# A feed-forward loop on one core: row statistics over pairs of rows, and 0.01 tanh added by VectorE instead of TensorE

## What is computed

```python
def step(h, _):
    h = h + 0.01 * jnp.tanh(h)
    h = h * jax.nn.sigmoid(h)
    h = _layernorm(h, ln_w, ln_b)
    h = jnp.einsum('bsc,dc->bsd', h, W) + b
    return (h, None)
x, _ = jax.lax.scan(step, _layernorm(h2), None, length=30)
out = h2 + x
```

## Time and profile before

| what | us |
|---|---|
| median of 3 runs | 2138.03 |
| lowest and highest of the 3 | 2136.45, 2356.8 |
| span of the profiled execution, first to last instruction | 2132.7 |
| last stage, from its first DVE operation to the span's end | 461.1 |

### The profile page before, as it was taken

The page is one execution under the profiler, slowest core; times in us unless marked ns, Lnnn a source line. Parts: engine busy times, 40 slices in busy tenths (PEclk is TensorE's granted clock), DMA queues, the critical chain, the costliest instruction groups (busy, mean ns, idle before and its releaser), DMA issues. The chain is left out here.

```text
span 2132.7 us, 61654 instructions
## 1 busy us (share of the span) xinstructions
PE 1903.4 (89%) x20166; PEld 1487.2 (70%) x20166; DVE 1674.5 (79%) x4836; ACT 1153.7 (54%) x2296; POOL 484.8 (23%) x431
## 2 busy tenths in 40 slices
PE   2316399999999999999999999999957799999998
PEld 2315277777777777777777777777747477777776
DVE  3205388888888888888888888888865788888887
ACT  0103266666666666666666666666614366666665
POOL 5000000000000000000000000000004699999997
PEclk9999699999999999999999999999987799999999
DMA  3333100000000000000000000000041100000000
GB/s 111 75 71 63 44 3 3 3 3 3 3 3 3 3 3 3 3 3 3 3 3 3 3 3 3 3 3 3 3 95 32 29 0 0 0 0 0 0 0 30
DMA packets 38153, 33.35 MB, mean 16 GB/s; under 512 B 13781, under 2 KB 35477, under 8 KB 37141
## 3 DMA queue, kind: packets, MB, share of 16 engines
q1 hardware_dynamic: 36159, 32.21, 6.4%
q10 hardware_dynamic: 1972, 0.86, 0.2%
HBM read 22.02 MB, written 11.03 MB: 15 GB/s over the span
## 5 line engine op out<-in xcount | busy, mean ns | idle before, releaser
L614 ACT ACTIVATE z1hi<-ps 128x375 f16<-128x375 f32 x820 | 398.7, 486 | 405.1 <-PE ps L556 405.1
L554 PE MATMUL ps<-AThi,y0hi 125*128 125x150 f16 x2460 | 567.1, 241 | 36.5 <-DVE z1lo L650 34.6
L555 PE MATMUL ps<-ATlo,y0hi 125*128 125x150 f16 x2460 | 584.9, 238 | 0.0
L650 DVE TENSOR_TENSOR z1lo<-ps,z1hi 128x375 f16<-128x375 f32 x820 | 445.8, 544 | 171.3 <-ACT z1hi L614 171.2
L556 PE MATMUL ps<-AThi,y0lo 125*128 125x150 f16 x2460 | 564.8, 239 | 0.0
L655 DVE TENSOR_TENSOR y<-ps,negb 125x384 f32<-125x384 f32 x820 | 451.1, 550 | 37.2 <-PE ps L571 37.2
L569 PE MATMUL ps<-W1hi,z1hi 128*128 128x128 f16 x2460 | 455.2, 219 | 0.2 <-DVE y L655 0.2
L571 PE MATMUL ps<-W1hi,z1lo 128*128 128x128 f16 x2460 | 454.1, 219 | 0.0
L570 PE MATMUL ps<-W1lo,z1hi 128*128 128x128 f16 x2460 | 453.6, 219 | 0.0
L645 DVE SCALAR_TENSOR_TENSOR y0lo<-ps,y0hi 125x512 f16<-125x512 f32 x615 | 420.7, 684 | 1.1 <-ACT y0hi L610 1.1
L610 ACT ACTIVATE y0hi<-ps 125x512 f16<-125x512 f32 x615 | 363.4, 591 | 13.4 <-PE ps L536 13.4
(11 more groups left out here) (197 smaller groups left out, 2315.4 us busy)
## 6 DMA issues: line engine op xcount, KB each, us to landing
pooled_parts<-stage SPq DMA_DIRECT2D x410, 4.0 KB
zk<-z_parts SPq DMA_DIRECT2D x16, 360.4 KB
parts<-pooled_parts SPq DMA_DIRECT2D x16, 256.0 KB, 5.7
xs<-in_x_v SPq DMA_DIRECT2D x3, 1201.2 KB
xs<-in_x_v SPq DMA_DIRECT2D x5, 720.7 KB
z_parts<-zp SPq DMA_DIRECT2D x20, 180.2 KB
pooled_parts<-stage SPq DMA_DIRECT2D x205, 2.0 KB
pooled_parts<-stage SPq DMA_DIRECT2D x205, 10.0 KB
```

Source lines behind the costliest of these rows:

```text
L554: nc.tensor.matmul(o, hi, ahi, start=(ph == 0), stop=False, skip_group_check=True)
L555: nc.tensor.matmul(o, hi, alo, start=False, stop=False, skip_group_check=True)
L614: nc.scalar.activation(z1hi[:, q, 0:GV], ps[:, Z1B + q % 2, 0:GV], ACT.Identity).then_inc(z1hi_done, 1)
L650: nc.vector.tensor_tensor(z1lo[:, q, 0:GV], ps[:, Z1B + q % 2, 0:GV], z1hi[:, q, 0:GV], ALU.subtract).then_inc(z1lo_done, 1)
```

## The change

The statistics of two rows are taken by one `bn_stats` over 128 numbers, read in turns from the one row and the other, so that the even places are the one row and the odd places the other. Its six numbers are then the two rows' own mean and sum of squared deviations, and one `tensor_scalar` adds 64 eps. The three small operations go, and `sm` in the first six steps. POOL has only the power left. The 0.01 tanh is added on DVE, in place in PSUM, between gn and the statistics of a step; PE's matmul with `pct` and `pct` itself go. `y_ready` becomes two semaphores, for even and odd chunks. The first waits of a buffer's reuse are put on other semaphores accordingly.

```diff
--- before.py
+++ after.py
@@ tokens @@
...
                 v_.memset(ones[:], 1.0)
-                v_.tensor_scalar(pct[:], ident[:], 0.01, None, ALU.mult)
...
@@ feed_forward @@
-        sm = sb("sm", [P, 2, CR])
-
-        bs, bs0 = (sb(f"bn_parts{i}", [P, 2, CR, 6]) for i in range(2))
-        dm, dm0 = (sb(f"dm_{i}", [P, 2, CR]) for i in range(2))
-        s2, s20 = (sb(f"s2_{i}", [P, 2, CR]) for i in range(2))
-        q2, q20 = (sb(f"q2_{i}", [P, 2, CR]) for i in range(2))
+        bs, bs0 = (sb(f"bn_pairs{i}", [P, 2, CP, 6]) for i in range(2))
...
-        y_ready = sem("y_ready")
+        y_ready = [sem("y_ready_even"), sem("y_ready_odd")]
...
+        def squares(pairs, b):
+            return pairs[:, b].rearrange("p j (i k) -> p (j i) k", i=2)[:, :, 2]
+
+        def means(pairs, b):
+            return pairs[:, b].rearrange("p j (i k) -> p (j i) k", i=2)[:, :, 1]
...
@@ gpsimd @@
-                def inverse_roots(s2, q2, var, rs, b, n, added, rooted):
-
-                    nc.gpsimd.tensor_tensor(var[:, b, :], s2[:, b, :], q2[:, b, :], ALU.add).then_inc(added, 1)
-                    pool.wait_ge(added, n + 1)
-                    nc.gpsimd.tensor_tensor(rs[:, b, :], var[:, b, :], expo[:], ALU.pow).then_inc(rooted, 1)
...
-                        pool.wait_ge(parts_done, 2 * n + 2)
+                        pool.wait_ge(var_done, n + 1)
                         if late(n, 2):
                             pool.wait_ge(gn_done, n - 1)
-                        inverse_roots(s2, q2, var, rs, b, n, var_done, rs_done)
+                        nc.gpsimd.tensor_tensor(rs[:, b, :], var[:, b, :], expo[:], ALU.pow).then_inc(rs_done, 1)
...
@@ scalar @@
-                            act.wait_ge(y_ready, s - 1)
+                            act.wait_ge(y_ready[c % 2], half(2) + 1)
...
-                        act.wait_ge(y_ready, n + 1)
+                        act.wait_ge(y_ready[cn % 2], half(1) + 1)
...
@@ tensor @@
-                    if on(0):
-                        pe.wait_ge(th_done, s + 1)
-                        nc.tensor.matmul(ps[:, c, :], pct[:], th[:, c % 2, :], start=False, stop=True,
-                                         skip_group_check=True).then_inc(y_ready, 1)
...
@@ vector @@
-                def statistics(bs, dm, s2, q2, b, n, diffs, made, bns):
-
+                def statistics(src, pairs, var, b, n, bns, made):
+
+                    for j in range(CP):
+                        last = v_.bn_stats(pairs[:, b, j, :], src[:, 2 * j:2 * j + 2, :].rearrange("p i d -> p d i"))
+                    last.then_inc(bns, 1)
                     dve.wait_ge(bns, n + 1)
-                    v_.tensor_tensor(dm[:, b, :], bs[:, b, :, 1], bs[:, b, :, 4], ALU.subtract).then_inc(diffs, 1)
-
-                    v_.scalar_tensor_tensor(s2[:, b, :], bs[:, b, :, 2], D * EPS, bs[:, b, :, 5], ALU.add,
-                                            ALU.add).then_inc(made, 1)
-                    dve.wait_ge(diffs, n + 1)
-                    v_.scalar_tensor_tensor(q2[:, b, :], dm[:, b, :], D / 4.0, dm[:, b, :], ALU.mult,
-                                            ALU.mult).then_inc(made, 1)
+                    v_.tensor_scalar(var[:, b, :], squares(pairs, b), D * EPS, None, ALU.add).then_inc(made, 1)
...
                     dve.wait_ge(h2_loaded, (c + 1) * 16)
                     if c >= 2:
-                        dve.wait_ge(var0_done, c - 1)
-                    for r in range(CR):
-                        last = v_.bn_stats(bs0[:, b, r, :], h2[:, c, r * D:(r + 1) * D])
-                    last.then_inc(bn0, 1)
-                    statistics(bs0, dm0, s20, q20, b, c, diff0, parts0_done, bn0)
-                    v_.tensor_tensor(sm[:, b, :], bs0[:, b, :, 1], bs0[:, b, :, 4], ALU.add).then_inc(sum_done, 1)
-                    dve.wait_ge(sum_done, c + 1)
-                    v_.scalar_tensor_tensor(x0c[:, b, :].rearrange("p (r d) -> p r d", d=D), spread(sm[:, b, :], P, CR),
-                                            -0.5, h2[:, c, :].rearrange("p (r d) -> p r d", d=D), ALU.mult,
-                                            ALU.add).then_inc(centred, 1)
+                        dve.wait_ge(rs0_done, c - 1)
+                        dve.wait_ge(centred, c - 1)
+                    statistics(rows, bs0, var0, b, c, bn0, var0_done)
+                    v_.tensor_tensor(x0c[:, b, :].rearrange("p (r d) -> p r d", d=D), rows,
+                                     spread(means(bs0, b), P, CR), ALU.subtract).then_inc(centred, 1)
...
                     if on(4):
...
+                    if on(0):
+                        dve.wait_ge(th_done, s + 1)
+                        v_.scalar_tensor_tensor(ps[:, c, :], th[:, c % 2, :], 0.01, ps[:, c, :],
+                                                ALU.mult, ALU.add).then_inc(y_ready[c % 2], 1)
                     if on(2):
                         n, cn, b = s - 2, (c - 2) % CH, c % 2
                         dve.wait_ge(g_done, n + 1)
                         if late(n, 2):
-                            dve.wait_ge(parts_done, 2 * n - 2)
-                        for r in range(CR):
-                            last = v_.bn_stats(bs[:, b, r, :], g_[:, cn % NG, r, :])
-                        last.then_inc(bn_done, 1)
-                    if on(2):
-                        n, b = s - 2, c % 2
-                        if late(n, 2):
-                            dve.wait_ge(var_done, n - 1)
-                        statistics(bs, dm, s2, q2, b, n, diff_done, parts_done, bn_done)
+                            dve.wait_ge(rs_done, n - 1)
+                        statistics(g_[:, cn % NG], bs, var, b, n, bn_done, var_done)
```

More of the change, by code:

```diff
@@ L686, in fuse @@
         bqk, bvrow = wcol[:, 0:2], wrow[:, 0, :]
-        pct = kept("pct", [P, P])
         ones = kept("ones_b", [P, P], BF16)
@@ L696, in fuse @@
         tokens(nc, ps, pooled_dram, txt, weights, W2s, b2row, ident, w4, wcol, wrow,
-               pct, ones, brow, h, mean, rstd)
+               ones, brow, h, mean, rstd)
         attention(nc, ps, h2_dram, h2r, h2_loaded, ident, wq, wk, wv, bqk, bvrow, h, mean, rstd)
-        feed_forward(nc, ps, h2r, h2_loaded, ident, wf, pct, ones, brow, out)
+        feed_forward(nc, ps, h2r, h2_loaded, ident, wf, ones, brow, out)
 def tokens(nc, ps, pooled_dram, txt, weights, W2s, b2row, ident, w4, wcol, wrow,
-           pct, ones, brow, h, mean, rstd):
+           ones, brow, h, mean, rstd):
     W4, w_cols, w_rows = weights
@@ L1114, in _, with feed_forward @@
                 steps(dve, body)
-def feed_forward(nc, ps, h2, h2_loaded, ident, wf, pct, ones, brow, out):
+def feed_forward(nc, ps, h2, h2_loaded, ident, wf, ones, brow, out):
     v_ = nc.vector
@@ L1208, in _, with body @@
                 pool.wait_ge(expo_made, 1)
[L1210 to L1214 removed]
                 def first(c):
                     if c < CH:
[L1218 removed]
+                        pool.wait_ge(var0_done, c + 1)
                         if c >= 2:
                             pool.wait_ge(x0_ready, c - 1)
[L1221 removed]
+                        nc.gpsimd.tensor_tensor(rs0[:, c % 2, :], var0[:, c % 2, :], expo[:], ALU.pow).then_inc(rs0_done, 1)
                 first(0)
[L1224 removed]
+                def body(s, c, on, half):
                     if on(2):
                         n, b = s - 2, c % 2
[L1227 removed]
+                        pool.wait_ge(var_done, n + 1)
                         if late(n, 2):
                             pool.wait_ge(gn_done, n - 1)
[L1230 removed]
+                        nc.gpsimd.tensor_tensor(rs[:, b, :], var[:, b, :], expo[:], ALU.pow).then_inc(rs_done, 1)
                 steps(pool, body, lambda s: first(s + 1))
@@ L1236, in _, with body @@
                 nc.scalar.activation(warm[:], ident[:, 0:1], ACT.Silu)
-                def body(s, c, on):
+                def body(s, c, on, half):
                     if on(0):
@@ L1303, in centre @@
                 def centre(c):
                     b = c % 2
+                    rows = h2[:, c, :].rearrange("p (r d) -> p r d", d=D)
                     dve.wait_ge(h2_loaded, (c + 1) * 16)
                     if c >= 2:
-                        dve.wait_ge(var0_done, c - 1)
-                    for r in range(CR):
-                        last = v_.bn_stats(bs0[:, b, r, :], h2[:, c, r * D:(r + 1) * D])
-                    last.then_inc(bn0, 1)
-                    statistics(bs0, dm0, s20, q20, b, c, diff0, parts0_done, bn0)
```

12 lines of the change are left out of this document (3 added, 9 removed).

## The result

The kernel after takes 2148.03 us (median of 13 runs), the kernel before took 2136.73 us in 13 runs beside it. The ratio is 1.0052, with a 95% interval of 1.004 to 1.0065: 11 us slower, and well inside the 2% that the forecast took as the limit of "same". The forecast was 2173 us (+1.6%). Rival A, where reading with a stride costs nothing, had said 2148. The highest run of before, 2356.8 us, was a slow one, and the ratio compares the others alone.

What follows compares the result with a forecast made beforehand. The loop PE, ACT, PE through gT (2.405 us a step) bounds before; afterwards VectorE at 2.55 us does. 174 x 0.145 = 25 plus 12 at the start gives +37 us, put at 2173 us (+1.6%), range 2145 to 2222.

Steps and rivals of the forecast that it cites:

- Rival A: The strided read is free, VectorE needs 2.26 us, only the start costs: +10, 2148 us; chance 0.28.
- the stride term: VectorE's bn_stats reading two rows in turns pays 0.56 ns an element, 0.29 us per chunk; bounds 0 and 1.05 ns.
- The rest of the VectorE sum: VectorE's steady step without the stride: gn, tanh addition, statistics and last small operation, 2.26 us.
- The tanh's addition in PSUM: VectorE's new in-place addition over 512 columns: 0.60 us, low end 0.58, high end 0.68.
- The bound: In steady steps, transposes, gT's copy on ACT and the next product form a loop of 2.405 us a step.
- L1286's removal: Taking the 0.01 tanh matmul off PE frees 0.86 us a step of its stream, worth 0.
- POOL's addition: POOL drops its addition and keeps the power, 1.64 to 2.16 us under a step of 2.405: no gain.
- The wait in the steady steps: VectorE's tanh addition waits for ACT's tanh, with some 1.5 us of slack before its silu: cost 0.
- The start: In the first six chunks VectorE waits for PE's copy and tanh: 12 us later, ten without the stride's cost.
- B: A whole extra cycle per strided element, or a dear PSUM write: step 2.79 us, +81, 2219 us; chance 0.20.
- C: PE stays at 1.2 GHz in the steady steps: loop 3.9 us, +273, 2411 us; chance 0.06.
- D: PE's stream was the bound, so steps fall to VectorE's 2.26 us: 2123 us; chance 0.03.

Runs made afterwards that it cites:

- experiment 1: The kernel after, but PE adds the 0.01 tanh in all chunks again; paired statistics and POOL's power alone stay: 2131.33 us, ratio 0.9966 to before.
- 4: The kernel after, but in the first six steps DVE scales its chunk before centring the next: 2140.6 us, ratio 1.0015 to before.
- Experiment 5b: The kernel before, with PE's transposes put ahead of bias and product: 2133.98 us, ratio 0.9977 to before.
- experiment 9: Two kernels as after, with single DVE operations added in the first stage to time strided and alternating reads; no whole-kernel time given.
- 5a: The kernel after, with PE's transposes put ahead of bias and product: 2158.11 us, ratio 1.0085 to before.
- 2: The kernel before, with DVE adding the 0.01 tanh but the old statistics and POOL's addition kept: 2218.92 us, ratio 1.0371 to before.
- experiment 6: The kernel after, with PE's transposes ahead of bias and product and DVE's tanh addition behind the statistics: 2109.78 us, ratio 0.987 to before.
- 7: As experiment 6, but DVE adds the tanh of odd chunks only and PE that of even ones: 2064.63 us, ratio 0.9652 to before.

## Why the forecast was wrong, point by point

**The step that failed** is the stride term: "I take 0.56, as it is the only strided row of this length. That adds 4 x 128 x 0.56 = 0.29 us per chunk". It measured 0: 281 ns in the kernel against 278 forecast without it, and 296 against 294 alone. The row behind it was read rightly (36 ns over 64 elements at 24 bytes in before, 40 here), but it shows another pattern. There every element lies on a new place. Here an access comes back after two elements to the row where it was. The low end of the bound, 0, was right, and the value above it was chosen by the only row there was, though that row was of another kind. With this term 25 of the forecast's 37 us go: VectorE's step is 2.22 us and not 2.55, so it stays under the loop's 2.4067 and does not become the bound.

**The rest of the VectorE sum** held: 2.26 without the stride, measured 2.22. The tanh's addition in PSUM was put at 0.60 and took 0.60. The slope of 1.05 ns an element came out at (281 - 211)/64 = 1.09.

**The bound.** "So the loop PE, ACT, PE alone costs 2.405 us, and L1286 now fills its hole": right. The step is 2.4067 in before, in after, with the tanh back on PE (1) and with the order of the start changed (4). L1286's removal was put at 0 and is 0; POOL's addition was put at 0 and is 0 (experiment 1, which drops it too). I read the drain for this, where the same hole shows without L1286. Experiment 5b shows how near it was: PE's own stream lies 0.003 us below.

**The wait in the steady steps** was put at 0. DVE does wait for the tanh at times, 10.1 us over 155 steps (the row of L1313 above); it costs nothing, since the loop leaves DVE 0.19 us a step (2.41 less 2.22).

**The start.** Forecast +12, or +10 without the stride; measured +11.4 for the whole stage. Inside, more was wrong than the sum shows. The wait window of 3.5 us is 3.48 (1684.72 to 1688.20). The centring was put at 1.95 and takes 1.59, the stride term once more (0.29) and 0.07 besides. The first product followed 35.8 us after DVE's first operation (its weights are loaded at 1711.48 us; the record of the bias matmul just ahead is missing), where 38 was forecast and 25.8 is the figure of before. So up to there the loss is 10 us, what the forecast had without the stride. What the sum left out comes behind it. From that product to the second copy of gT after takes 2.56 us and before 1.74, because the granted clock rose only within 1712 to 1716 us, in the middle of this product, where in before it had risen by then: 0.8 us. The end of the stage holds 0.6 more, which I did not follow up; 10, 0.8 and 0.6 make the 11.4. The 3.2 us between the first two copies of gT are thus only in part the clock's. Some 1.4 lie on the way from the sixth x0 through PE's copy of it and the product (5.17 us against 3.78), and 1.8 are DVE's, which makes this x0 1.25 us behind the start of the first copy of gT, and not 0.54 ahead of it as in before.

**The rivals.** A is what happened. That it named 2148 to the unit is in part luck: its start was 1.4 us too short, and the 2138 it was added to lies 1.3 us above the later median of before. B, a whole cycle or a dear write to PSUM: no, 281 ns and 0.60 us. C, the clock: it stood at 0.50 until 37.5 us after the stage's start (20.5 in before), and then at 1.00 in the steady steps with PE at 70%, so it cost the start something and the steps nothing. What the Trainium skill (TensorE: Matmul & The Clock Gate, section "Part 4: PE-mode transpose") says of transposes, on which the forecast drew for C, no run here shows, as none has transposes alone. D, PE's stream as the bound: refuted by the step of after and of experiment 1.

## What to carry to other kernels

When work is taken from a full engine, look for a place in the same trace where that work is absent, here the drain: if the period stays, something else of equal length stands behind, and only both together, order and load, bring the gain (here 2.407 to 2.219, then 1.974 us). A wait added to an engine that works in order belongs behind all that is ready, and a pipeline's first rounds are to be costed by themselves: six steps of 180 were the whole loss. A price for a strided read should be taken from a row with the same order of accesses; where there is none, "costs nothing" belongs in the working beside the nearest row, and a few single operations in a stage that has room would have priced it beforehand, as experiment 9 did afterwards.

## What was unexpected

- Turns between two places in SBUF cost VectorE nothing, between four they cost 0.64 ns an element (82 ns over 128); 64 elements at a step of 16 bytes or more cost 0.6 to 0.7 ns each (38 to 44 ns).
- A turn of the hardware loop costs about half a microsecond (0.48 in 5a; (2.79 - 2.70) x 6 = 0.54 in 2) where DVE's last operation ahead of it is a short one, and nothing in 6 and 7, where the 0.60 us of the tanh come last.
- POOL's power takes 1.64 us if it starts ahead of gn, and more if gn is already running: 2.16 us at 0.02 us behind gn's start (before), 2.02 at 0.17 (after and the rows of 5a's kernel below), 1.94 at 0.25 (5a). In each case that is 1.64 from a point 0.54 to 0.55 us behind gn's start. Beside the running 0.01 tanh, which has one input in SBUF and one in PSUM, it stays at 1.64. With the power first, gn starting 0.45 us into it stays at 0.68 us and the power at 1.64 (experiment 6, 1901.82 and 1902.27).

```profile
1902.19 0.69 DVE L1309 TENSOR_TENSOR gn<-g,rs 128x512 f32<-128x512 f32 x1
1902.36 2.02 POOL L1214 TENSOR_TENSOR rs<-var,expo 128x8 f32<-128x8 f32 x1 [0.53 <-DVE var L1278]
```

The Trainium skill (SBUF — State Buffer, section "Who interferes with whom") says that a VectorE instruction with both inputs in SBUF, as gn is, contends with a GpSimd instruction that reads SBUF. With gn first the rows agree: POOL loses 0.30 to 0.52 us, as much as is left of gn's first 0.54 us. With the power first neither is held up.
